# The first attention layer of a four-layer model: both normalisations' scalings on GpSimd, and a new table of places for every step

## What is computed

```
q  = layer_norm(x^T   + positions, g_q,  b_q)      # first normalisation, queries
kv = layer_norm(ctx^T + positions, g_kv, b_kv)     # and keys/values
Q, K, V = q @ Wq, kv @ Wk, kv @ Wv                 # 16 heads of 8
y  = softmax(Q K^T / sqrt(8)) V @ Wo
r  = y + q
h  = layer_norm(r, g_ffn, b_ffn)                   # second normalisation
out = gelu(h @ W1 + b1) @ W2 + b2 + r
```

## Time and profile before

| | before |
|---|---|
| median of the runs | 2195.7 us |
| the profiled execution's own time | 2197.88 us |
| its span in the profile | 2195.9 us |
| PE busy | 2077.2 us, 95% |
| DVE busy | 1483.7 us, 68% |
| ACT busy | 1281.1 us, 58% |
| POOL busy | 647.8 us, 30% |
| layer 0's attention, in the timeline | 0 to 327 us |

### The profile page before, as it was taken

How to read it: one execution, slowest core, us unless ns; L and a number is a source line. 1 busy time by engine, 2 the same in 40 slices (tenths; PEclk the granted TensorE clock), 3 DMA queues, 4 the chain that set the end, 5 groups by cost and what they waited for, 6 DMA issues and landing times. The chain is left out here.

```text
span 2195.9 us, 47492 instructions
## 1 busy us (share of the span) xinstructions
PE 2077.2 (95%) x17700; PEld 1727.5 (79%) x17700; DVE 1483.7 (68%) x2828; ACT 1281.1 (58%) x3304; POOL 647.8 (30%) x661
## 2 busy tenths in 40 slices
PE   6999979999898899999999999999998999999899
PEld 4666656888687788888888888888887877776678
DVE  5788854555454666666677766666676359999953
ACT  3777763566653544545455545445455458888853
POOL 4444321111124413030303312030102136677711
PEclk9999998999999999999999999999999999999999
DMA  4000001000102223232322323232223020000000
GB/s 135 16 18 14 2 5 55 2 2 2 34 7 68 87 78 111 82 111 81 101 92 87 99 82 108 83 102 74 71 71 144 1 60 2 2 2 2 2 13 27
DMA packets 119007, 117.16 MB, mean 53 GB/s; under 512 B 6656, under 2 KB 91136, under 8 KB 117760
## 3 DMA queue, kind: packets, MB, share of 16 engines
q1 hardware_dynamic: 118784, 114.13, 16.3%
HBM read 78.72 MB, written 35.39 MB: 52 GB/s over the span
## 5 line engine op out<-in xcount | busy, mean ns | idle before, releaser
L866 ACT ACTIVATE l_probs<-l_s_psum,l_neg_max 128x129 f32<-128x129 f32 x512 | 182.9, 364 | 300.6 <-DVE l_neg_max L948 300.6
L953 DVE SCALAR_TENSOR_TENSOR l_context_low<-l_c_psum,cols,l_context_high 128x512 fp32r<-128x512 f32 x128 | 95.9, 749 | 185.8 <-ACT l_context_high L861 185.5
L1505 DVE TENSOR_REDUCE l_neg_max<-l_psum 128x2 f32<-128x512 f32 x256 | 163.5, 683 | 50.1 <-PE l_psum L1295 49.7
L690 POOL TENSOR_TENSOR l_head_w_high<-l_head_raw,one 128x768 fp32r<-128x768 f32 x30 | 44.7, 1489 | 482.2 <-PE l_t_psum L823 447.8
L2576 POOL TENSOR_TENSOR l_probs<-l_probs,l_mask_add 128x512 f32<-128x512 f32 x128 | 161.7, 1285 | 76.7 <-DVE l_probs L2804 76.7
L1434 ACT ACTIVATE l_PT<-l_psum 128x512 f32<-128x512 f32 x256 | 132.2, 603 | 56.9 <-PE l_psum L1323 56.9
L2746 ACT ACTIVATE l_probs<-l_probs,l_neg_max 128x128 f32<-128x128 f32 x512 | 159.8, 396 | 5.5 <-DVE l_neg_max L2811 5.1
L805 PEld LDWEIGHTS l_c_psum<-l_PT,values 128*128 128x128 f32 x1024 | 135.3, 194 | 19.1 <-DMA l_PT<-l_moving 8.0
L805 PE MATMUL l_c_psum<-l_PT,values 128*128 128x128 f32 x1024 | 137.3, 278 | 6.1 <-DMA l_PT<-l_moving 6.1
L782 PE MATMUL l_s_psum<-l_KT,l_QT 128*128 128x129 f32 x1024 | 135.1, 274 | 2.4 <-issue 1.6
L973 DVE TENSOR_TENSOR x<-x,l_o_psum 128x512 f32<-128x512 f32 x128 | 87.9, 686 | 68.4 <-PE l_o_psum L823 68.2
(11 more groups left out here) (328 smaller groups left out, 6352.6 us busy)
## 6 DMA issues: line engine op xcount, KB each, us to landing
l_moving<-l_turned SPq DMA_DIRECT2D x127, 256.0 KB, 2.0
l_PT<-l_moving SPq DMA_DIRECT2D x508, 64.0 KB
l_head_raw<-in_l_heads SPq DMA_DIRECT2D x32, 384.0 KB, 4.7
l_w<-in_l_w SPq DMA_DIRECT2D x4, 1024.0 KB, 10.3
l_ctx_in<-in_ctx_T SPq DMA_DIRECT2D x16, 256.0 KB, 5.6
l_value_raw<-in_l_values SPq DMA_DIRECT2D x8, 512.0 KB, 5.1
l_value_rows<-in_l_rows SPq DMA_DIRECT2D x8, 512.0 KB, 5.9
l_x_in<-in_x_T SPq DMA_DIRECT2D x16, 128.0 KB, 2.3
```

The source lines that it names most:

```text
L866: last = act.activation(probs[:, i, :], scores[:, i // 2, i % 2, :], ACT.Exp, bias=neg_max[:, i:i + 1], scale=1.0, accum_out=den[:, i:i + 1])
L953: dve.scalar_tensor_tensor(out=context[1][:, :], in0=c_bank[:, :], scalar=vector("bias_v", s), in1=context[0][:, :].bitcast(F32), op0=ALU. ...
L1505: dve.tensor_reduce(neg_max[:, u % 2, qt, at:at + 2], bank[:, :].rearrange("p (e k) -> p e k", e=2), AX, ALU.max, negate=True).then_inc(fr ...
```

## The change

Two kinds of work move to GpSimd, and every number in `AT0` is replaced.

1. `scaled` leaves ACT. POOL makes it with four `tensor_scalar` instructions, (x - mean) times rstd, with mean and rstd read from memory for each partition. The two instructions for the shift, its tile and its two semaphores go.
2. `scaled_b` leaves DVE. POOL makes it with two such instructions.
3. `stats_b` of batch u waits until batch u - 2 is scaled on POOL, where it waited for that batch's rstd.
4. The table. Lines behind it are renumbered: a PE step's line is 10 higher in the new kernel.

```
 AT0 = {
-    "place": (-5.54,),
+    "place": (-3.651,),
...
-    "score": (-0.54, -0.22, 0.04, 0.16),
+    "score": (-0.5042, -0.2299, 0.0067, 0.2733),
...
                 inverse_root(pool, c, rstd_part, u, mean_var[:, u % 2, :, 1:2], rstd[:, u % 2, :, :], 1e-5, 4)\
                     .then_inc(rstd_done, 1)
-                pool.tensor_scalar(out=shift[:, u % 2, :, :], in0=mean_var[:, u % 2, :, 0:1], scalar1=-1.0, scalar2=None,
-                                   op0=ALU.mult).then_inc(mean_turned, 1)
+
+            def scaled(u):
                 pool.wait_ge(rstd_done, u + 1)
-                pool.wait_ge(mean_turned, u + 1)
-                pool.tensor_tensor(out=shift[:, u % 2, :, :], in0=shift[:, u % 2, :, :], in1=rstd[:, u % 2, :, :],
-                                   op=ALU.mult).then_inc(shift_done, 1)
+                if u >= 2:
+                    filled(pool, "normed", u - 2)
+                for i in range(4):
+                    last = pool.tensor_scalar(out=xn[:, u % 2, i, :], in0=x_in[:, u % 4, i, :],
+                                              scalar1=mean_var[:, u % 2, i, 0:1], scalar2=rstd[:, u % 2, i, :],
+                                              op0=ALU.subtract, op1=ALU.mult)
+                last.then_inc(xn_done, 1)
...
+            def scaled_b(u):
+                pool.wait_ge(rstd_b_done, u + 1)
+                if u:
+                    filled(pool, "renormed", u - 1)
+                for qt in range(2):
+                    last = pool.tensor_scalar(out=rn[:, qt, :], in0=r[:, u % 2, qt, :],
+                                              scalar1=mean_var_b[:, u % 2, qt, 0:1], scalar2=rstd_b[:, u % 2, qt, :],
+                                              op0=ALU.subtract, op1=ALU.mult)
+                last.then_inc(rn_done, 1)
...
-            def scaled(u):
-                act.wait_ge(shift_done, u + 1)
...
                 if u >= 2:
-                    dve.wait_ge(rstd_b_done, u - 1)
+                    dve.wait_ge(rn_done, u - 1)
...
-            def scaled_b(u):
-                dve.wait_ge(rstd_b_done, u + 1)
```

More of the change, by code:

```diff
@@ L1032 @@
-    "parts": (-1.21,),
-    "neg_T": (-0.64,),
-    "neg_T_a": (-0.15,),
-    "score": (-0.54, -0.22, 0.04, 0.16),
[L1036 to L1051, removed]
+    "place": (-3.651,),
+    "stats": (-3.3265,),
+    "root": (-2.0031,),
+    "scaled": (-1.9934,),
+    "normed": (-2.3486,),
+    "normed_a": (-2.2412,),
+    "project": (-1.6335,),
+    "project_a": (-1.5549,),
+    "round": (-0.7957,),
+    "blocks": (-0.4326,),
+    "value": (-1.1937,),
+    "values": (-1.0269,),
+    "rows": (-1.4939, -1.4734, -1.4418, -1.2732, -1.2628, -1.219, -1.2025, -1.0549, -1.0479, -1.0059, -0.8986, -0.8664, -0.8087, -0.7974, -0.7153, -0.6505),
@@ new lines @@
+    "maximum": (-1.2006, -1.1924, -1.1199, -1.1185, -1.0926, -1.0701, -1.0659, -0.9038, -0.8552, -0.7952, -0.7917, -0.7634, -0.7083, -0.6072, -0.4933, -0.4911),
+    "parts": (0.1956,),
+    "neg_T": (-0.5691,),
+    "neg_T_a": (-0.5014,),
+    "score": (-0.5042, -0.2299, 0.0067, 0.2733),
+    "exponents": (-0.4574, -0.373, -0.261, -0.2478, -0.0768, -0.0317, -0.0156, 0.028, 0.0816, 0.1856, 0.2064, 0.2312, 0.3517, 0.3952, 0.3991, 0.441),
+    "context": (0.163, 0.4763),
+    "slots": (0.2951, 0.5361),
@@ L1052 @@
+    "untangle": (0.5382, 1.1534),
+    "share": (0.8737, 1.2552),
+    "context_T": (1.2617,),
+    "turned_T": (1.3191,),
+    "out": (1.3502,),
+    "added": (1.6101,),
+    "back": (1.3723,),
+    "back_a": (1.5156,),
+    "stats_b": (2.271,),
+    "root_b": (2.9977,),
+    "scaled_b": (3.2834,),
+    "renormed": (2.8497,),
+    "renormed_a": (3.0282,),
 }
@@ L1107, in attention0 @@
         rstd = sb("rstd", [P, 2, 4, 1])
-        shift = sb("shift", [P, 2, 4, 1])
         xn = sb("xn", [P, 2, 4, P])
@@ L1141, in attention0 @@
         rstd_part, rstd_done, xn_done = sem("rstd_part"), sem("rstd_done"), sem("xn_done")
-        mean_turned, shift_done = sem("mean_turned"), sem("shift_done")
         blocks_done, blocks_rounded = sem("blocks_done"), sem("blocks_rounded")
@@ L1248, in root_b @@
                     .then_inc(rstd_b_done, 1)
-            order.run({"place": place, "root": root, "blocks": make_blocks, "round": round_blocks, "parts": neg_parts_of,
-                       "root_b": root_b})
+            def scaled_b(u):
[7 more added lines that the diff above has]
+                last.then_inc(rn_done, 1)
+            order.run({"place": place, "root": root, "scaled": scaled, "blocks": make_blocks, "round": round_blocks,
+                       "parts": neg_parts_of, "root_b": root_b, "scaled_b": scaled_b})
             clear_stale(pool, c)
@@ L1463, in renormed @@
                                bias=c.col("l0_ffn_b", 0), scale=c.col("l0_ffn_g", 0)).then_inc(free, 1)
-            order.run({"scaled": scaled, "normed_a": normed, "project_a": project, "neg_T_a": neg_turned, "exponents": exponents, "slots": slots_of,
+            order.run({"normed_a": normed, "project_a": project, "neg_T_a": neg_turned, "exponents": exponents, "slots": slots_of,
                        "turned_T": turned_T, "back_a": back, "renormed_a": renormed})
@@ L1539, in stats_b_of @@
                 last.then_inc(var_b_done, 1)
-            def scaled_b(u):
-                dve.wait_ge(rstd_b_done, u + 1)
[L1543 to L1550, removed]
             order.run({"stats": stats_of, "values": values, "maximum": maximum,
-                       "share": share, "added": added, "stats_b": stats_b_of,
-                       "scaled_b": scaled_b})
+                       "share": share, "added": added, "stats_b": stats_b_of})
 AT1 = {
```

## The result

| | before | changed |
|---|---|---|
| median of 5 runs each | 2193.41 us | 2204.33 us |
| lowest to highest | 2191.55 to 2197.38 | 2202.05 to 2206.01 |
| ratio, 95% interval | | 1.0041 [1.0025, 1.0056] |
| the profiled execution, its span | 2197.88, 2195.9 | 2202.05, 2200.2 |
| POOL busy, whole program | 647.8 us | 712.6 us |

Here the medians are 10.9 us apart (1.0050 by them alone). The forecast was 2194.5, with a range from 2187.5 to 2202.0: the changed kernel's median of 2204.33 lies above it, that of the second measurement, 2198.0, within it.

The account below looks back on a forecast made before the run. Two chains were taken to bound the turn: score, exponents, score, and the maxima up to neg_T. Turns -0.6, start +0.9, end -1.5 sum to -1.2 us, from 2195.7 to 2194.5; range 2187.5 to 2202.

Parts of the forecast that it names:

- The price on POOL: One scaling on POOL was taken at 0.6 us, with ends 0.31 and 0.965; six a turn make 3.6 us.
- The price on DVE: DVE's scaling pass was read as 0.79 us against POOL's 0.31 to 0.56 for its like, against the skill's rule.
- POOL in that turn: Four scalings behind root_b end at 14.8, parts due at 15.1; fits by 0.3, breaks at 0.68 a scaling.
- rival A: Parts wait for POOL's scalings, delaying neg_T and S0: 1.1 us a turn in 15 turns, +17, 2211; chance 0.12.
- The new turn without POOL: Steady turn on PE from S0 to S0: 17.73, taken as 17.8 for 17.84; -0.6 us in fourteen turns.
- Rival C: Late row costs S1 and S2 nothing: S0 to S2 7.06, turn 17.53, -4.3 in fourteen turns, 2191; chance 0.08.
- D: Rival: rows 4 or rows 9 hold S1 or S2 by 0.3 us a turn, +4, 2199; chance 0.08.
- Relief of ACT and DVE: Scalings taken off ACT (1.65 us) and DVE (two of 0.79) each turn stand in no chain: no steady gain.
- The start: Up to batch 1's S0: first S0 at 34.5 for 35.20, then +1.6 for value and rows; +0.9 us together.
- rival B: TensorE's clock is up sooner as the new order fills PE's gaps, first context under 3 us: 2189; chance 0.14.
- The end: Attention's end: last back copied earlier -2.55, scalings on POOL +0.6, untangle 1 +0.5; -1.5 us together.

Follow-up runs that it names:

- second measurement: The changed kernel and the kernel before, both unedited, run again: 2198.0 us (12 runs) against 2192.33 (17 runs), ratio 1.0027 [1.0017, 1.0038].
- scaled sooner: Changed kernel with two table numbers (root, scaled) moved so POOL's four scalings run ahead of root_b: turn 17.93, 0.9999 [0.9980, 1.0017] of the kernel before.
- new table alone: Kernel before with the changed table but for two numbers, scalings still on ACT and DVE: turn 17.93, 0.9991 [0.9973, 1.0009] of the kernel before.
- old table with the scalings on POOL: Changed kernel's code with the table of before, but two numbers placing the scalings where POOL was idle: turn 17.84, 1.0013 [0.9996, 1.0029] of before.
- scaled_b back on DVE: Changed kernel with scaled_b's code of before and table number 2.7, only scaled's move remaining: turn 18.25, one run, 2204.20 us.
- the last variant: Scaled sooner, with the last batch but two's renormed transposes put ahead of the last context: turn 17.93, 1.0012 [1.0002, 1.0021] of the kernel before.

## Why the prediction was wrong, step by step

- **The price on POOL: this step failed.** I put 0.6 between rows of 0.31, 0.56 and 0.965 and it is 0.78. With two constants it is 0.62 in this place, near the 0.56 of the row with one constant; the row with two had 0.31, and no run shows why the same form takes twice that here. I had noted that two operands from memory are unlike either row and given it no cost. The room was small: 0.1 more would just have been covered, 0.18 was not. Of the steady loss of 4.75 us, 3.55 is this term. With it the attention stands 3.1 to 3.4 us over before's in the two pairs of profiles; less what it cost in the turns, it would stand some 0.1 to 0.7 under. By the prediction's own sum, 0.78 for 0.6 gives 4 x 0.10 x 15 = +6 and 2200.5: the side of the outcome, but not the 10.9 us of the first measurement, most of which no step of mine and no run explains.
- **The price on DVE: misread.** I took 0.79 for the pass on DVE and concluded that POOL was no dearer. That row is a mean of unlike passes. In a steady turn of before the two take 1.68 and 0.34, and the long one lasts as long as POOL's `round`, which reads 128x1024 elements beside it; in the last turns, with POOL idle, the pair takes 0.60. View of L1546 from 160 to 170 us (count, least, median and greatest ns), then timelines of POOL and DVE, all of the kernel before:

```profile
L1546 DVE SCALAR_TENSOR_TENSOR l_rn<-l_r,l_mean_var_b,l_rstd_b x2: 337/1010/1682, 163.3 to 164.9; 128x128 f32<-128x128 f32 x2
...
162.90 1.90 POOL L1228 TENSOR_TENSOR l_blocks_round<-l_Q,shapes 128x1024 fp32r<-128x1024 f32 x1
...
269.11 0.60 DVE L1546 SCALAR_TENSOR_TENSOR l_rn<-l_r,l_mean_var_b,l_rstd_b 128x128 f32<-128x128 f32 x2
```

  So POOL's 0.78 is 2.3 times an undisturbed pass on DVE. This misreading cost the sum nothing, but it is what spoke against the dearer price.
- **POOL in that turn: right, and closer than it had to be.** Forecast from S0: root_b at 11.4, scalings from 12.4, parts due at 15.1, breaking point 0.68. Measured: 11.53, 12.49, 15.25 (scaled sooner), 0.70. The mechanism of rival A, to which I gave 0.12, is shown by one edit each way: without the scalings there 17.93, with one more 19.02. Its sign, no idle time of POOL ahead of the parts, was met. Its price was 0.32 a turn in 11 turns, not 1.1 in 15.
- **The Trainium skill's rule** (GPSIMD Engine Reference, section 4.1: elementwise work belongs on VectorE, GpSimd being about twice as slow with two inputs). My estimate of 1.6 by it was twice the measured 0.78, because I doubled the mixed mean 0.79; doubling the undisturbed 0.34 gives an estimate of 0.68, the breaking point itself. The same table row calls one-input operations roughly line-rate. POOL's `tensor_scalar` reads one tensor and two scalars a partition, and was 2.3 times as slow as DVE's pass all the same. At 1.6 the changed kernel would have lost 3.6 a turn.
- **The new turn without POOL: 17.8, measured 17.93.** S0 to S1 3.54 for 3.53; S1 to S2 3.75 for 3.73; S2 to S3 4.79 for 4.69 (untangle 1 holds PE 0.59 instead of 0.49); S3 to S0 5.85 for 5.78, where PE waits 0.21 for `added`, which I had said ends before. In 14 turns that is +1.2 where I had -0.6. Rival C is out, and D did not show: S1 and S2 came within 0.02 of their times.
- **Relief of ACT and DVE brings nothing: right**, by the old table with the work moved.
- **The start: +0.9, measured -2.2 and -1.3.** The first S0 was foreseen: 34.5 for 35.20 (-0.7), measured -0.96 and -0.72. The 1.6 us for value and rows at half pace were wrong: at half pace S0 to S1 is 4.68 in both kernels (35.20 to 39.88; 34.24 to 38.92), so that extra work fills waits. The remainder is the clock's moment, as rival B had it. B's sign, a first context under 3 us, was met (2.33 and 1.93), but B's cause, the filled gaps, is not shown: the old order had 1.93 too.
- **The end: -1.5, measured -0.55** in the pair in which the clock held up to the last transposes. Last back_a after S3 is 3.34 for 6.02 (-2.68; I said -2.55), S0 to S3 +0.59 (+0.5), but back_a to the feed-forward is +1.54 where I had +0.6. Of these, 0.97 are the scalings' pair (1.58 for 0.61), and 0.38 a wait that I had not seen: POOL's last scaled_b stands behind the transposes of the batch ahead, which now stand behind the last context.

Timelines of ACT, POOL and PE at the end of the changed kernel's second profile, to be read against the earlier trace rows:

```profile
321.95 0.42 ACT L1457 ACTIVATE l_r<-l_psum 128x256 f32<-128x256 f32 x1
...
324.62 1.58 POOL L1255 TENSOR_SCALAR l_rn<-l_r,l_mean_var_b,l_rstd_b 128x128 f32<-128x128 f32 x2 [0.38 <-PE l_psum L1386]
...
326.25 0.60 PE L1386 MATMUL l_psum<-ident,l_rn 128*128 128x128 f32 x2 [1.81 <-POOL l_rn L1255]
329.56 0.80 PE L114 MATMUL l_mlp_psum<-l_mlp_n_high,l_mlp_w_high 128*128 128x512 f32 x1 [2.70 <-POOL l_mlp_w_low L370]
```

**What stays open.** The attention is 3.1 to 3.4 us longer in both pairs of profiles; the medians differ by 5.7 and 10.9. The remainder of the program, the same instructions, took from 1859.8 us (changed, second profile) to 1872.1 (scaled_b on DVE) in these eleven profiles, so scatter of this size hides in single executions. Part of it can be placed. In three of the eleven (new table alone, old table with the scalings on POOL, scaled_b back on DVE) TensorE's granted clock was 0.66 to 0.70 from 33 to 38 us after the feed-forward's first matmul, where the other eight have 1.00, and layer 1's first rows came 41.6 to 42.0 us after that matmul instead of 39.2 to 39.8. Another part lies at the attention's end (last section). And over the twelve runs of the new table alone the time follows the mean granted clock, from 2185.28 us at 0.988 to 2198.36 at 0.980. It may not be all: scaled sooner reached the feed-forward 1.8 to 4.5 us ahead of before's two profiles (324.68 for 326.51 and 329.17) and the last variant 2.1 to 4.7, yet their medians lie 0.8 and 2.4 over before's; the new table alone was 1.0 to 3.7 ahead and its median 1.2 under. Whether scalings on POOL cost 2 or 3 us behind the attention, or chance does, no run here tells. The profiles give no sign of it: the remainder averages 1866.2 us in the eight with scalings on POOL and 1867.4 in the three without.

## What to carry to other kernels

When work is moved to an engine that is mostly idle, its queue's order counts, not its load: POOL stood at 13.8 of 20 us and still held up TensorE, because the work was put between a late step and a small urgent one. Two numbers of a table took the wait away, though the kernel was then only as fast as before. Where a chain has 0.3 us of room, a price taken from a like operation is not enough: the kind of operand (constant or from memory) was worth more than the room, so the forecast should weigh the outcome by which side of the breaking point each candidate price falls on, and not by the middle of them. And a group's mean is no price until its least and greatest are known: 0.79 was made of 0.34 and 1.68.

## What the runs showed of the hardware

- **`tensor_scalar` on GpSimd**, 128x128 float32: 0.78 us with two operands for each partition from memory, 0.62 with two constants in the same place (one run); in the last layer a form with two constants took 0.31. The same 3.1 us for four were taken at 9.35 us, in the first batch:

```profile
9.35 3.14 POOL L1207 TENSOR_SCALAR l_xn<-l_x_in,l_mean_var,l_rstd 128x128 f32<-128x128 f32 x4
```

- **DVE's `scalar_tensor_tensor` beside POOL's `round`** took 1.68 us for 0.34, while POOL's `tensor_tensor` took 1.90 (rows in the section above). With the new table and the scalings still on DVE, the long pass took 1.99 and `round` 2.06. That the one holds up the other is read from their times; no run separates them.
- **The moment at which TensorE goes from 1.2 to 2.4 GHz** moved by 8 us and more between two executions of the kernel before: a quarter's first matmuls took 0.71 instead of 1.24 from 39.53 us on in one, and not before the first context, at 47.04, was over in the other. In the changed kernel's first profile it rose within the context at 46.49, which took 2.33; with scaled sooner at 38.93. In both first profiles the view of busy times granted 1.00 from 30 to 60 us; this half pace is seen in durations alone.
- **The clock also falls at the attention's end**, in some executions. There PE idles 1.57 and 1.79 us ahead of S1 and S2, for exponents, in both profiles of the changed kernel. In the first the window from 310 to 320 us was granted 0.85, and the context took 2.70 for 1.93; in the second, 1.00 and 1.93. S2 to S3 took 5.69 for 4.11, which covers the 1.4 us between the two ends (23.52, 22.12). The 5.69 came in five of the eight profiles with the new table and in none of the three with the old (3.53 each), where PE idles 1.35 and 1.57 us there. So the new order may cost 1.6 us at the end in some executions; nothing was run to settle it.

```profile
318.80 2.70 PE L1346 MATMUL l_psum<-l_PT,l_V 128*32 128x256 f32 x32
...
310.00:320.00 10.00, 6.64 (x82) 3.73 (x78) 1.50 (x7) 6.65 (x13) 0.00 (x0) 0.85 0.01 2
```
